# ScalarE instead of VectorE builds part of the one-hot matrices of an edge-counting loop

## The reference, cut to what matters

```python
edge_index = jnp.stack([src, dst])
h = jnp.maximum(_layernorm(x, axis=-1), 0.0)
x = x + attention(h, edge_index, Wq, bq, Wk, bk, Wv, bv)   # a * adj + (1 - adj) * NEG, softmax, @ v
h = jnp.maximum(_layernorm(x, axis=-1), 0.0)
x = x + gcn(h, W1, b1, gamma, beta, W2, b2, edge_index)    # segment sums over edges and self loops
```

## Time and profile before

| | us |
|---|---|
| median of 3 runs (310.0 to 310.64) | 310.06 |
| the profiled execution's own time | 310.67 |
| its span in the profile | 308.9 |
| PE busy | 297.6 (96%) |
| DVE busy | 210.3 (68%) |
| ACT busy | 143.8 (47%) |
| POOL busy | 57.3 (19%) |

### The profile page before, as it was taken

The page is one execution under the profiler, slowest core; times in us unless marked ns, Lnnn a source line. Parts: engine busy times, 40 slices in busy tenths (PEclk is TensorE's granted clock), DMA queues, the critical chain, the costliest instruction groups (busy, mean ns, idle before and its releaser), DMA issues.

```text
span 308.9 us, 4793 instructions
## 1 busy us (share of the span) xinstructions
PE 297.6 (96%) x1345; PEld 229.6 (74%) x1345; DVE 210.3 (68%) x471; ACT 143.8 (47%) x245; POOL 57.3 (19%) x95
## 2 busy tenths in 40 slices
PE   8998979899999999999999999999999999999995
PEld 7876436465665688888888888888788888878884
DVE  2878999999998748667657484767444388276311
ACT  3889943443455626635464445437622035243000
POOL 5254370000000260032121311203010044100000
PEclk9999999999999999999999999999999999999999
DMA  7707040000410216643643825133102000000221
GB/s 269 291 13 195 1 136 2 1 0 3 159 44 3 47 24 176 130 96 58 122 87 83 151 47 111 36 68 65 37 7 63 1 2 0 0 2 0 100 107 68
DMA packets 42311, 21.66 MB, mean 70 GB/s; under 512 B 35760, under 2 KB 36016, under 8 KB 42288
## 3 DMA queue, kind: packets, MB, share of 16 engines
q1 hardware_dynamic: 41744, 20.33, 26.4%
q10 hardware_dynamic: 544, 1.05, 0.9%
HBM read 10.88 MB, written 2.10 MB: 42 GB/s over the span
## 4 chain that ended last, share of the span: by engine, by line
PE 78%; DVE 8%; ACT 5%; issue 3%; DVEq 3%; DMA 1%; POOL 1%; ACTq 0%; POOLq 0%
PE ps L950 18%; PE ps L952 17%; PE ps L951 17%; PE ps L1200 9%; PE ps L1123 8%; PE ps L1016 6%; DVE src_oh L671 3%; PE ps L984 2%; DMA qk_raw<-L_gnn_Wk_in 1%; DVE dst_oh L673 1%; DVEq L671 1%; ACT T L428 1%; POOL lnc L351 1%; ACT T L423 1%; ACT WT L459 1%
## 5 line engine op out<-in xcount | busy, mean ns | idle before, releaser
L671 DVE TENSOR_SCALAR src_oh<-iota,ecol 128x512 f16 x149 | 44.5, 352 | 4.3 <-issue 3.2
L1016 PE MATMUL ps<-src_oh,dst_oh 128*128 x149 | 37.8, 382 | 5.2 <-DVE dst_oh L673 5.0
L1016 PEld LDWEIGHTS ps<-src_oh,dst_oh 128*128 x149 | 14.4, 104 | 25.4 <-issue 16.3
L1123 PE MATMUL ps<-cnt,qh 128*128 128x512 f32 x128 | 30.0, 391 | 0.3 <-ACT cnt L541 0.3
L1200 PE MATMUL ps<-qh,cnt 128*128 128x512 f32 x128 | 29.3, 390 | 0.0
L443 ACT ACTIVATE cnt<-ps 64x512 int16<-64x512 f32 x32 | 18.9, 592 | 20.7 <-PE ps L1030 20.3
L1123 PEld LDWEIGHTS ps<-cnt,qh 128*128 128x128 f32 x128 | 23.9, 188 | 5.6 <-DVE qh L829 0.7
L1200 PEld LDWEIGHTS ps<-qh,cnt 128*128 128x128 f32 x128 | 23.9, 188 | 5.3 <-DVE vb L931 0.3
L952 PE MATMUL ps<-v,pT 128*128 128x512 f32 x64 | 25.0, 390 | 0.0
L950 PE MATMUL ps<-hT,qh 128*128 128x512 f32 x64 | 24.9, 389 | 0.0
L950 PE MATMUL ps<-v,pT 128*128 128x512 f32 x64 | 24.9, 389 | 0.0
(11 more groups left out here) (178 smaller groups left out, 665.6 us busy)
## 6 DMA issues: line engine op xcount, KB each, us to landing
xt<-x_in SPq DMA_DIRECT2D x16, 256.0 KB, 3.2
out<-xt SPq DMA_DIRECT2D x8, 256.0 KB, 2.1
qk_raw<-L_gnn_Wk_in ACTq DMA_DIRECT2D x2, 512.0 KB, 4.7
qk_raw<-L_gnn_Wq_in SPq DMA_DIRECT2D x2, 512.0 KB, 6.6
wB_raw<-L_gnn_Wv_in SPq DMA_DIRECT2D x2, 512.0 KB, 8.8
wB_raw<-L_gnn_W_in SPq DMA_DIRECT2D x2, 512.0 KB, 3.7
w_raw<-L_gnn_W_in SPq DMA_DIRECT2D x2, 512.0 KB, 4.2
bias_row<-L_gnn_b_in SPq DMA_DIRECT2D x2, 256.0 KB, 3.8
```

Of the source, the lines that this page charges most:

```text
L671: dve.tensor_scalar(src_oh[:, bass.ds(slot, 1), j, :].rearrange("p a n -> p (a n)"), iota[:, :], ecol[:, bass.ds(c + j, 1)], None, ALU.is_ ...
L1016: m = pe.matmul(ps[:, i % 2, :], dst_oh[:, bass.ds(slot, 1), :, j].rearrange("p a n -> p (a n)"), src_oh[:, bass.ds(slot, 1), j, :].rearra ...
L1123: m = pe.matmul(bank(g), qh[:, d, a, c * P:(c + 1) * P], cnt[:, d, n * HALF:(n + 1) * HALF], start=(d == 0 and a == 1), stop=last)
```

## The change

From group 3 on (`ACT_LEADS` = 3), DVE no longer makes `src_oh` for the two straight chunks of a group. ACT makes them into a tile `lead_oh` of its own (two buffers, in the place of `adj`, which is not in use yet): two activations Abs of 512 columns, which give |iota - source|, and after a wait for both one Relu of 1024 columns, relu(1 - |iota - source|). This is issued for group i+2 right after `counts(i)`; for group 3 it stands after the last layer norms of `hrow`, before `counts(2)`. PE waits for `lead_made` before the matmuls of a group and takes the moving operand of the first two from `lead_oh`. POOL makes the bias columns: once the negated sources `ncol`, and then 13 times a load of the group's bounds into a register and a copy of two columns into `lead_col`; this stands between `ln1(6)` and the last eight `drel`.

```diff
+ACT_LEADS = 3
-    adj = sb("adj", [P, ADJ, N], I16)
+    adj, lead_oh = shared([("adj", [P, ADJ, N], I16)], [("lead_oh", [P, 2, LEAD, HALF], BF16)])
+        def lead_columns(i):
+            bounds = pool.value_load(lohi[0:1, ORDER[i]:ORDER[i] + 1], min_val=256, max_val=257 * NCH)
+            pool.tensor_copy(lead_col[:, i, :], ncol[:, bass.ds(bounds & (NCH - 1), LEAD)]).then_inc(S["lead_cols"], 1)
-        pool.wait_ge(S["ecol_ready"], 1)
+        pool.wait_ge(S["ecol_ready"], 2)
...
         ln1(6)
+        pool.tensor_scalar(ncol[:, :], ecol[:, :], -1.0, 0.0, ALU.mult,
+                           ALU.add).then_inc(S["ncol_ready"], 1)
+        pool.wait_ge(S["ncol_ready"], 1)
+        pool.wait_ge(S["bounds_ready"], 1)
+        for i in range(ACT_LEADS, NW):
+            lead_columns(i)
         for i in range(8, NW):
             targets_of(i)
...
+        def lead_onehots(i):
+            n = i - ACT_LEADS + 1
+            act.wait_ge(S["lead_cols"], n)
+            for j in range(LEAD):
+                act.activation(lead_oh[:, i % 2, j, :], iota[:, :], ACT.Abs,
+                               bias=lead_col[:, i, j:j + 1]).then_inc(S["lead_dist"], 1)
+            act.wait_ge(S["lead_dist"], LEAD * n)
+            act.activation(lead_oh[:, i % 2, :, :], lead_oh[:, i % 2, :, :], ACT.Relu, bias=ones[:, 0:1],
+                           scale=-1.0).then_inc(S["lead_made"], LEAD)
...
             if i == 2:
                 for t in range(KC, NT):
                     layer_norm(t)
+                lead_onehots(ACT_LEADS)
             counts(i)
...
+            if ACT_LEADS < i + 2 < NW:
+                lead_onehots(i + 2)
...
-        def chunks_of(i, c, count):
+        def chunks_of(i, c, count, src=True):
...
-            for j in range(count):
+            for j in range(count if src else 0):
...
-            chunks_of(i, first, LEAD)
+            chunks_of(i, first, LEAD, i < ACT_LEADS)
...
                 m = pe.matmul(ps[:, i % 2, :], dst_oh[:, bass.ds(slot, 1), :, j].rearrange("p a n -> p (a n)"),
+                              lead_oh[:, i % 2, j, :] if first and i >= ACT_LEADS else
                               src_oh[:, bass.ds(slot, 1), j, :].rearrange("p a n -> p (a n)"), start=first and j == 0,
...
+            if i >= ACT_LEADS:
+                pe.wait_ge(S["lead_made"], LEAD * (i - ACT_LEADS + 1))
```

More of the change, by code:

```diff
@@ L100, in gnn_kernel @@
     cnt16 = sb("cnt16", [P, NT, NT, P], I16)
-    adj = sb("adj", [P, ADJ, N], I16)
+    adj, lead_oh = shared([("adj", [P, ADJ, N], I16)], [("lead_oh", [P, 2, LEAD, HALF], BF16)])
+    hold("region_adj", 4)
     xt = sb("xt", [P, XT, D], F32)
@@ L119, in gnn_kernel @@
     bias_row = sb("bias_row", [P, 2, D], F32)
+    ncol = sb("ncol", [P, NCH + PAD], F32)
+    lead_col = sb("lead_col", [P, NW, LEAD], F32)
+    ones = sb("ones", [P, 1], F32)
     ident = sb("ident", [P, P], F32)
@@ L159, in gnn_kernel @@
     x_sums x_means x_squares ln_coef h_ready item_ps item_hi item_lo uw_ready hw_second fill_ready
-    onehots onehots_used c_done c16 loops_added adj_in0 adj_in1 adj_in2 adj_in3
+    ncol_ready lead_cols lead_dist lead_made onehots onehots_used c_done c16 loops_added adj_in0 adj_in1 adj_in2 adj_in3
     deg_ready degm_ready degm_ps flag_ready dinv_ready
@@ L333, in _ @@
         pool.memset(half_pow[:, :], -0.5)
+        pool.memset(ones[:, :], 1.0)
         pool.wait_ge(S["ident_ready"], 1)
```

## The result

The changed kernel is 0.7% slower: 312.65 us (median of 4, 312.26 to 313.21) against 310.03 us (4 runs, 309.83 to 310.64) on the same chip; ratio 1.0071, 95% interval 1.0046 to 1.0096. The forecast was 309.7 with a range that ended at 312.4.

What follows compares the result with a forecast made beforehand. PE bounds the loop where items carry it, DVE where groups follow closely. From 310.67 profiled, -0.2 (groups 3 to 15) and -0.25 (POOL), about -0.4, give 310.3, or 309.7 against the median; range 307.8 to 312.4.

Steps and rivals of the forecast that it cites:

- the price of a lead: ACT's time for two Abs, a wait and a Relu, per group: 2.40 us, bounds 2.2 and 2.7.
- the restart of PE behind its new waits: At groups 14 and 15, PE starts 0.22 us after the end of ACT's last lead instruction.
- rival 1: ACT's unbroken chain of ten leads is dearer, kernel slower: 1.0 us per 0.1 a lead, 2.6 gives 311.7; chance 0.23.
- The place: ACT's unbroken chain of ten leads from group 4's counts; PE waits in groups 14 and 15, 1.5 to 2 us each.
- DVE's relief: Two src_oh fewer per group, 0.52 us each group, 6.8 over thirteen; gives back 2.7 us by group 13.
- rival 2: ACT keeps pace, all waits on DVE go, q(1,0) starts at 99.7: -3.5 us, with POOL 306.3; chance 0.15.
- One lead: 0.61 + 0.71 + 0.04 + 1.04 = 2.40 us: On ACT, per group: two Abs 0.61 and 0.71, wait 0.04, Relu to the next start 1.04.
- The other members of the chain: ACT's work between leads: ten counts 15.2 us, six plain copies 2.9, four q copies 2.3.
- the extra waits of PE ... cost nothing: PE's added waits for leads were taken as free, since its queue runs ahead behind the items.
- POOL's part: Column copies push the last eight drel from group 2 to group 3; group 2 ends 0.25 us sooner, bounds 0 and 0.5.
- the queues: ACT's copies come 1 to 4 us later; only q1 and q2 come close, where DVE has slack.

Runs made afterwards that it cites:

- kept-busy kernel: The changed kernel with PE making 32 small zero matmuls before its lead waits in groups 14 and 15: 311.24 us, ratio 1.0038; changed kernel 313.41 on that chip.

## Why the prediction was wrong

Three steps of it failed: the price of a lead, the restart of PE behind its new waits, and the clock behind them, which had no term at all. What happened is rival 1 and more: its rule gives 311.6 for a lead of 2.59, and the time was 312.65.

**Right.** The place: ACT's chain runs unbroken from group 4 on, and PE loses its lead again in groups 14 and 15, where it waits 2.15 and 1.59 us (forecast: 1.5 to 2 each). DVE's relief takes away PE's waits for DVE in groups 6 to 13. Its size was somewhat high: counted from the end of group 2, PE closes group 13 2.14 us earlier, not 2.7, most of the difference because of the `drel` in group 4; and with zeros for ACT's work the whole gain is 2.74 us, where rival 2 had 3.5. ACT's chain covers this difference.

The reason given for rival 1, that this work is cheaper on DVE, was right too: the two `src_oh` cost DVE 0.52 us and ACT 2.59. By the Trainium skill's rule to keep relu-like work on VectorE (page "ScalarE: Activation LUTs", section "Rules for kernel authors") the change loses; with leads for 13 groups the measurement sides with it, and with leads for nine groups it does not.

**Wrong, the price of a lead.** The step "One lead: 0.61 + 0.71 + 0.04 + 1.04 = 2.40 us" measured 2.59: the last term is 1.17, since nothing overlaps the Relu, and the wait 0.09. (The 1.04 was itself between the rows, which had 1.02 and 1.06.) Ten times 0.19 is 1.9 us. The other members of the chain were a little shorter than costed (20.0 us instead of 20.4), so lead 15 was done 45.97 us after the counts of group 4 and not 44.5: +1.5. The price lay within my bounds of 2.2 to 2.7, but rival 1, which it makes true, was given 0.23.

**Wrong, "the extra waits of PE ... cost nothing".** I took 0.22 us from an end to PE's start and 1.12 for group 15, rows of a PE whose queue had run ahead. Behind a wait that blocks, the first matmul comes 0.44 us after the Relu's end (96.68 to 97.12 for lead 14, 101.52 to 101.96 for lead 15), and the next set starts 0.81 to 0.84 us after the first matmul, where it is 0.45 in group 13. The rows call the idle time "issue"; that it is the register instructions of the group is my reading of the program. At full clock, in the kept-busy kernel, group 15 takes 1.53 us from its first matmul to q(1,0). In the chain the last wait counts: 0.22 + 0.41, +0.63.

**Missing, the clock.** I forecast two waits of PE of 1.5 to 2 us close together and priced them by their length alone. With the lower clock group 15 took 2.17 us from its first matmul to q(1,0) instead of 1.53, and the first five matmuls of q(1,0) 2.16 instead of 1.23: +1.57, the part of the kept-busy kernel's 1.67 that is clock.

Sum of the misses: 1.5 + 0.63 + 1.57 = 3.7, less 0.3 for POOL's part (0.55 where I took 0.25). That is 3.4 from the forecast -0.45 to the measured +2.95. That all of POOL's part reaches the time is luck: the `drel` went to group 4, not 3, and there they cost DVE time, which ACT's chain happened to cover.

**Half right, the queues.** I saw that the copies of q1 and q2 would come late to DVE "where DVE has slack". DVE got them at 88.1 and 93.0 in the trace and idled 0.88 and 1.99 us for them, and in the changed kernel PE's wait for ACT covered it. It shows only when leads 14 and 15 are taken away: leads 3 to 13 gained 1 us of the 3.

## What to carry to other kernels

Before work is moved to an engine with idle time, put its whole queue in a row and ask which of its older duties stand behind the new work; where the row has no gap left, move the work for those stages only in which the relieved engine is the bound, and make late pieces early, in gaps that the row shows. A wait that an engine like PE did not have before costs more than its length: here 0.63 us for the restart behind it and 1.57 for the clock.

## What the runs showed of the hardware that I had not expected

- Behind two waits of 2.15 and 1.59 us (94.98 to 97.12 and 100.37 to 101.96), with 0.37 us of work in 100 to 102, the granted clock was 0.68 in 102 to 104 and 0.50 (1.2 GHz) in 104 to 106; matmuls of 512 columns were then 0.43 us apart instead of 0.23. With small matmuls in the waits it stayed at 1.00. Whether one of the two waits alone would have done it, no run shows.
- PE's first matmul came 0.44 us after the end of the Relu it had waited for, at both waits and in both profiles of the changed kernel; with small matmuls ahead of the wait it was 0.34.
- An activation that follows the Relu starts 0.02 us behind its end, many others about 0.10 us ahead of the end; the increment is not the reason.
- A register load on POOL ahead of a copy of two columns makes 0.72 us for the pair.
- The first 8 transposes took 1.97, 1.40 or 1.09 us in different executions while the granted clock was 1.00.
